# Second attention of a two-block network: the score products for the row maxima run for two heads at once, in two halves of TensorE's rows

## What is computed

```python
qkv = x @ Wqkv
q, k, v = jnp.split(qkv, 3, axis=-1)            # (4, 512, 256) each
q = q.reshape(b, s, 16, 16)                     # 16 heads of 16
q = q / (sqrt(mean(q * q)) + EPS) * scale_q     # one mean over everything
k = k / (sqrt(mean(k * k)) + EPS) * scale_k
attn = softmax(einsum('bqhd,bkhd->bhqk', q, k))
z = einsum('bhqk,bkhd->bqhd', attn, v)
x = x + z.reshape(b, s, 256) @ Wo
```

## Time and profile before

| | us |
|---|---|
| median of 3 runs | 1603.98 (1602.13 to 1608.87) |
| profiled execution | 1612.12, span 1610.3, mean granted TensorE clock 0.947 |
| busy: PE, PEld, DVE | 1461.8 (91%), 999.7, 1066.7 |
| busy: ACT, POOL | 855.1, 477.2 |
| first tall tile of rounds 0, 1, 2 | 938.00, 953.38, 966.78 |
| value products of round 1 begin at | 956.48, 959.75, 963.03, 965.78 |
| first tall tile of the last round, its last value products | 1149.89, 1161.75 |

### The profile page before, as it was taken

One profiled execution on the slowest core, in us unless ns is written; L12 is line 12 of the kernel. 1 busy time (PEld: TensorE's weight loads), 2 busy tenths in 40 slices (PEclk: granted clock), 3 DMA queues, 4 the chain that ended last, 5 costly groups with the idle time before them and its releaser, 6 DMA issues.

```text
span 1610.3 us, 20214 instructions
## 1 busy us (share of the span) xinstructions
PE 1461.8 (91%) x7408; PEld 999.7 (62%) x7420; DVE 1066.7 (66%) x1216; ACT 855.1 (53%) x1511; POOL 477.2 (30%) x140
## 2 busy tenths in 40 slices
PE   5898797589898999997999889999899999999997
PEld 3576342289797978753444333333368888888886
DVE  6996496579899898864443567777355565565655
ACT  2433466499889898631343268777624333333332
POOL 0999110069888888400321320000000000000000
PEclk7899899789999999979999999999978999999999
DMA  6110010402222111402112122442000000000000
GB/s 266 35 48 1 1 53 21 178 27 85 100 105 106 66 66 41 161 2 39 44 36 78 50 81 59 138 137 92 1 1 0 1 14 1 1 14 1 13 1 14
DMA packets 36624, 87.61 MB, mean 54 GB/s; under 512 B 8350, under 2 KB 24948, under 8 KB 32948
## 3 DMA queue, kind: packets, MB, share of 16 engines
q1 hardware_dynamic: 36532, 86.39, 16.1%
HBM read 68.10 MB, written 18.21 MB: 54 GB/s over the span
## 4 chain that ended last, share of the span: by engine, by line
PE 55%; ACT 2%; DVE 2%; issue 2%; DVEq 1%; ACTq 0%
PE ps L1418 13%; PE ps L1427 12%; PE ps L1288 4%; PE ps L1155 3%; PE ps L1330 3%; PE ps L1276 2%; PE ps L1181 2%; PE ps L1117 2%; ACT arena L1851 1%; PE ps L987 1%; PE ps L580 1%; PE ps L1313 1%; PE ps L1039 1%; PE ps L1189 1%; PE ps L1167 1%
## 5 line engine op out<-in xcount | busy, mean ns | idle before, releaser
L2500 POOL TENSOR_TENSOR arena<-arena 128x2048 f32<-128x2048 f32 x63 | 287.3, 4579 | 167.1 <-DVE arena L2059 166.8
L2059 DVE TENSOR_TENSOR_SCAN arena<-arena,ps 128x1024 f32<-128x1024 f32 x128 | 284.2, 2271 | 44.9 <-ACT arena L1694 22.3
L1418 PE MATMUL ps<-arena 128*128 128x256 f32 x896 | 216.7, 388 | 3.2 <-DVE early L2445 1.8
L1418 PEld LDWEIGHTS ps<-arena 128*128 128x128 f32 x896 | 173.1, 195 | 30.3 <-DVE early L2445 3.0
L1694 ACT ACTIVATE arena<-arena,mam 128x511 f32<-128x511 f32 x256 | 166.1, 712 | 34.3 <-DVE arena L2059 34.3
L1851 ACT ACTIVATE arena<-ps,rho 128x512 f32<-128x512 f32 x256 | 158.3, 689 | 27.7 <-PE ps L1330 26.5
L2291 DVE TENSOR_REDUCE mxs<-ps 128x1 f32<-128x512 f32 x224 | 141.1, 684 | 44.9 <-PE ps L1276 43.1
L975 PE MATMUL ps<-early,arena 128*128 128x128 f32 x768 | 129.7, 277 | 18.1 <-DVE arena L2059 17.8
L1884 ACT ACTIVATE hT<-hT,arena 128x256 f32<-128x256 f32 x192 | 85.5, 500 | 86.7 <-DVE hT L2449 55.1
L2480 POOL TENSOR_TENSOR arena<-arena 128x4096 f32<-128x4096 f32 x16 | 115.0, 7189 | 43.6 <-DVE arena L1978 43.6
L1682 ACT ACTIVATE arena<-arena,early 128x512 f32<-128x512 f32 x192 | 124.0, 711 | 0.1
(11 more groups left out here) (344 smaller groups left out, 2328.5 us busy)
## 6 DMA issues: line engine op xcount, KB each, us to landing
arena<-bc_scratch SPq DMA_DIRECT2D x32, 512.0 KB, 3.7
arena<-in_ffn SPq DMA_DIRECT2D x8, 1024.0 KB, 4.9
batch_scratch<-arena SPq DMA_DIRECT2D x2, 3072.0 KB, 9.1
arena<-batch_scratch SPq DMA_DIRECT2D x6, 1024.0 KB, 6.8
arena<-q_scratch SPq DMA_DIRECT2D x96, 64.0 KB, 2.2
arena<-k_scratch SPq DMA_DIRECT2D x96, 64.0 KB, 2.2
arena<-in_dec_w SPq DMA_DIRECT2D x1, 3855.0 KB, 16.4
arena<-in_cond SPq DMA_DIRECT2D x1, 3739.5 KB, 11.5
```

The costliest lines, as they stand in the source:

```text
L1418: done = pe.matmul(ps[:, bank, i * S // 2:(i + 1) * S // 2], weights[:, f, :], x, start=first and i == 0, stop=last and i == 1, skip_group ...
L2059: dve.tensor_tensor_scan(half, view(decay[:, (2 * k + h) % 3], [[1, 2 * S]]), view(ps[:, FEED + 2 * h, :], [[1, 2 * S]]), 0.0, ALU.mult, A ...
L2500: pool.tensor_tensor(state[:, k % SLOTS], state[:, k % SLOTS], view(c_rows[:, j % 2, k % G, :], [[0, M], [1, S]]), ALU.mult).then_inc(s_hc, 1)
```

## The change

- A short product takes three of the six part pairs, 48 rows (`MAIN`). Heads of even number have these in rows 0 to 47, heads of odd number in rows 64 to 111, so that two heads' products can stand in the two row halves of TensorE.
- The other three pairs lie in the other half, from row 65 for even heads and from row 1 for odd ones (`PART_ROWS`); the maxima's row is 64 for even heads and 0 for odd ones (`MAX_ROW`). A tall product takes rows 0 to 112 (`TALL` = 113), the gaps being zero.
- The three early stacks keep the old order, and all their pairs.
- In `attend` the order is two tall tiles, then both short ones, with one wait ahead of them: for the maximum two before the first of them.
- `load_heads` needs two DMAs for a block of 16 rows, one for the even and one for the odd heads: 24 for 12 in a stack, each of half the bytes. The maxima's row is two DMAs for one.
- GpSimd writes, for each of the four stacks in `qstack` and `kstack`, rows 32 to 63 and 96 to 127 with zeros in q and k, and the rows of -1 in k (`constant_rows`), after its split of the last k: first for the fourth group, for which SP now waits (`s_ones` 2) ahead of its load, then for the others, for which it waits (`s_ones` 5) ahead of the first load of batch 1.

```diff
+MAIN = 3 * DH
+TALL = P // 2 + 1 + MAIN
+MAX_ROW = (P // 2, 0)
+PART_ROWS = ((0, DH, 2 * DH, P // 2 + 1, P // 2 + 1 + DH, P // 2 + 1 + 2 * DH),
+             (P // 2, P // 2 + DH, P // 2 + 2 * DH, 1, 1 + DH, 1 + 2 * DH))
...
+        def is_early(b, hg):
+            return isinstance(b, int) and b == 0 and hg < 3
+
+        def heads_loaded(b, hg):
+            return len(Q_PARTS) * 2 * 16 * (2 * b + (1 if hg < 3 else 2))
...
+                    for odd in range(2):
+                        at = PART_ROWS[odd][j]
+                        queue.dma_start(of_parity(stack, odd)[at:at + DH],
+                                        bass.AP(src.tensor, src.offset + off + odd * DH * row,
+                                                [[row, DH], [2 * DH * row, HG // 2], [1, S]])
+                                        ).then_inc(s_heads[hg], 16)
...
-            sp.dma_start(stacks_of(0, 0)[0][STACK:STACK + 1], mrow[0:HG, 0, :]).then_inc(s_mrow_in, 16)
+
+            def max_rows_in(b, hg):
+                for odd in range(2):
+                    sp.dma_start(max_row_of(b, hg, odd), mrow[odd:HG:2, hg % 2, :]).then_inc(s_mrow_in, 16)
+
+            max_rows_in(0, 0)
             store_parts(B - 1)
+            sp.wait_ge(s_ones, 2)
             load_heads(sp, 0, HG - 1, Q_STACK, K_STACK)
...
                         if b == 0 and hg == 0:
                             sp.wait_ge(s_q_out, 16 * B + 1)
                             sp.wait_ge(s_k_out, 16 * B + 1)
+                            sp.wait_ge(s_ones, 5)
...
-                i, qc = s % HG, s // HG
+                qc = s // HG
                 if s == 0:
-                    pe.wait_ge(s_heads[hg], (b + 1) * 2 * len(Q_PARTS) * 16)
-                pe.wait_ge(s_max, (b * HG + hg) * 16 + s + (1 if hg + s == 0 else -1))
+                    pe.wait_ge(s_heads[hg], heads_loaded(b, hg))
+                pe.wait_ge(s_max, (b * HG + hg) * 16 + s + (1 if hg + s == 0 else 0))
                 q, k = stacks_of(b, hg)
-                pe.matmul(ps[:, (hg + s) % 3, :], q[0:STACK, i, qc * P:(qc + 1) * P], k[0:STACK, i, :],
-                          start=True, stop=True).then_inc(s_s_mm, 1)
+                for odd in range(2):
+                    i = s % HG + odd
+                    low = 0 if is_early(b, hg) else odd * P // 2
+                    rows_in = slice(low, low + (STACK if is_early(b, hg) else MAIN))
+                    pe.matmul(ps[:, (hg + s + odd) % 3, :], q[rows_in, i, qc * P:(qc + 1) * P], k[rows_in, i, :],
+                              start=True, stop=True).then_inc(s_s_mm, 1)
...
-                            pe.matmul(ps[:, 3 + (hg + n) % 3, :], k[0:STACK + 1, i, kc * P:(kc + 1) * P],
-                                      q[0:STACK + 1, i, :], start=True, stop=True).then_inc(s_t_mm, 1)
-                            if not (final and hg >= 2):
-                                scores(*ahead, n)
+                            tall = STACK + 1 if is_early(b, hg) else TALL
+                            pe.matmul(ps[:, 3 + (hg + n) % 3, :], k[0:tall, i, kc * P:(kc + 1) * P],
+                                      q[0:tall, i, :], start=True, stop=True).then_inc(s_t_mm, 1)
+                        if not (final and hg >= 2):
+                            scores(*ahead, 4 * kc + 2 * pair)
...
-            minus_row(kstack[:, HG - 1]).then_inc(s_ones, 1)
+                last = minus_row(stack)
+            last.then_inc(s_ones, 1)
             pool.drain()
             split_parts(pool, B - 1, kf, last_kp, rest_q, s_kf, s_k_out, s_kp)
-            for hg in range(HG - 1):
-                last = minus_row(kstack[:, hg])
-            last.then_inc(s_ones, 1)
+
+            def constant_rows(hg):
+                for low in (P // 4, 3 * P // 4):
+                    for stack in (qstack, kstack):
+                        pool.memset(view(stack[low:low + P // 4, hg], [[1, HG * S]]).bitcast(F32), 0.0)
+                for odd in range(2):
+                    at = MAX_ROW[odd]
+                    last = pool.memset(of_parity(kstack[:, hg], odd)[at:at + 1].bitcast(F32), minus_ones)
+                last.then_inc(s_ones, 1)
+
+            pool.wait_ge(s_qp, B + 1)
+            constant_rows(HG - 1)
+            pool.wait_ge(s_vs, B + 1)
+            pool.wait_ge(s_q_out, 16 * B + 1)
+            pool.wait_ge(s_k_out, 16 * B + 1)
+            for hg in range(HG - 2):
+                constant_rows(hg)
+            constant_rows(HG - 2)
```

More of the change, by code:

```diff
@@ L467, in stacks_of, with of_parity, max_row_of @@
         def stacks_of(b, hg):
-            if isinstance(b, int) and b == 0 and hg < 3:
+            if is_early(b, hg):
                 return early_q[hg], early_k[hg]
             return qstack[:, hg], kstack[:, hg]
+        def is_early(b, hg):
+            return isinstance(b, int) and b == 0 and hg < 3
+        def heads_loaded(b, hg):
+            return len(Q_PARTS) * 2 * 16 * (2 * b + (1 if hg < 3 else 2))
+        def of_parity(stack, odd):
+            return stack.rearrange("p (j o) s -> p j o s", o=2)[:, :, odd]
+        def max_row_of(b, hg, odd):
+            at = STACK if is_early(b, hg) else MAX_ROW[odd]
+            return of_parity(stacks_of(b, hg)[0], odd)[at:at + 1]
         va, at = carve(at, TILES, H * SLOT)
@@ L631, in load_heads @@
                     off = (hg % 2) * HG * DH * row + part * C * S + (hg // 2) * S
-                    queue.dma_start(stack[j * DH:(j + 1) * DH],
-                                    bass.AP(src.tensor, src.offset + off, [[row, DH], [DH * row, HG], [1, S]])
-                                    ).then_inc(s_heads[hg], 16)
+                    if is_early(b, hg):
+                        queue.dma_start(stack[j * DH:(j + 1) * DH],
+                                        bass.AP(src.tensor, src.offset + off, [[row, DH], [DH * row, HG], [1, S]])
+                                        ).then_inc(s_heads[hg], 16)
+                        continue
+                    for odd in range(2):
[3 more added lines that the diff above has]
+                                                [[row, DH], [2 * DH * row, HG // 2], [1, S]])
+                                        ).then_inc(s_heads[hg], 16)
         @block.sync
@@ L772, in feed @@
                         sp.wait_ge(s_mrow, g + 3)
-                        row = stacks_of(b + (hg + 1) // HG, nxt)[0]
-                        sp.dma_start(row[STACK:STACK + 1], mrow[0:HG, nxt % 2, :]).then_inc(s_mrow_in, 16)
+                        max_rows_in(b + (hg + 1) // HG, nxt)
                     if not last:
@@ L1322, in attend @@
                     ahead = (b + (hg + 2) // HG, (hg + 2) % HG)
-                    pe.wait_ge(s_mrow_in, 16 * (g + 1) + 1)
+                    pe.wait_ge(s_mrow_in, 32 * (g + 1) + 1)
                     for j in range(8):
@@ L1368, in _ @@
             attend(0, True, False)
-            pe.wait_ge(s_ones, 2)
+            pe.wait_ge(s_ones, 5)
             with pe.Fori(1, B - 1) as b:
@@ L1839, in max_row @@
                 act.wait_ge(s_m_tr, g + 1)
-                act.wait_ge(s_mrow_in, 16 * g - 15)
+                act.wait_ge(s_mrow_in, 32 * g - 31)
                 act.activation(mrow[:, parity, :], ps[0:HG, 7, :], ACT.Copy).then_inc(s_mrow, 1)
@@ L2529, in _ @@
             for stack in early_k:
-                minus_row(stack)
-            minus_row(kstack[:, HG - 1]).then_inc(s_ones, 1)
+                last = minus_row(stack)
+            last.then_inc(s_ones, 1)
             pool.drain()
             split_parts(pool, B - 1, kf, last_kp, rest_q, s_kf, s_k_out, s_kp)
-            for hg in range(HG - 1):
-                last = minus_row(kstack[:, hg])
-            last.then_inc(s_ones, 1)
+            def constant_rows(hg):
[14 more added lines that the diff above has]
+            constant_rows(HG - 2)
             pool.drain()
```

## The result

The changed kernel takes 1619.93 us (median of 10 runs, 1611.52 to 1632.17), the kernel before 1603.76 (10 runs, 1599.94 to 1608.87): ratio 1.0103, 95% interval 1.0073 to 1.0133. It is slower by 16 us.

What follows compares the result with a forecast made beforehand. In the second attention, ScalarE bounds each round's first and last quarters, TensorE the middle two. Start stall 6.5, half clock 2.0 and steady rounds 2.7 sum to +11.2 us on 1604.0: 1615.2, 8 in 10 within 1606 to 1627.

Steps and rivals of the forecast that it cites:

- The likeliest case: Whole kernel: start stall, half clock and slower steady rounds add 11.2 us, giving 1615.2; chance 0.52, own range 1610 to 1621.
- The start stall: Second attention, before round 1: SyncE waits for GpSimd's constants, then issues 24 DMAs, so the first tall product starts 6.5 us later.
- The stage is the same in both: Step from profiled execution (1612.1 us) to median run (1604.0): the second attention was taken as equal, so 11.2 us was added unchanged.
- Half clock in round 1: Round 1 of the second attention, after TensorE's idle time: clock at 0.50 adds 2.0 us, from 0 to 2.4.
- Steady: Rounds 3 to 15 of scores: joint wait for maxima and 0.09 us edges add 0.23 us a round, 2.7 us in all.
- Later rows of maxima: Later rounds of the second attention: SyncE's longer loads stay hidden; rows 0.2 late in two rounds, at most 0.5 us, taken as 0.
- The slack of 0.8 us: SyncE's queue in later rounds: load and maxima row take 15.1 us, 15.9 are available, so at least 0.8 us remains.
- the rival with 0.62: SyncE's loads: each issue costs 0.62 us, SyncE becomes the bound, +20 us, 1639; chance 0.06.
- one after the other: Short-product pairs on TensorE: the two halves run in sequence, not side by side, +11.4 us, 1626.6; chance 0.13.
- Edges free: TensorE between full and half rows: shape changes cost nothing, -5.3 us in the rounds, 1607.2 in all; chance 0.16.
- the cheaper start: Start of the second attention: half loads issue in 0.36 us and the clock holds for half, 1611.6; chance 0.09.
- the full gain: TensorE's short products: 22.7 us less, with 8.5 us lost at the start, comes through, 1589.8; chance 0.04.

Runs made afterwards that it cites:

- half_alone: Changed kernel in the old order, tall and short products alternating, each 48-row short product alone with its own wait: 1654.7 us, ratio 1.0317 to the kernel before.
- before_again: The kernel before, unchanged, run for a second trace: its profiled execution took 1600.10 us.
- split_loads: The kernel before with only the change's DMAs: 24 of 32 KB for 12 of 64 KB per stack, two per maxima row: 1614.1 us, ratio 1.0044.
- order_only: The kernel before with only the new order, two tall products, then two full 96-row short ones behind one joint wait: 1602.1 us, ratio 0.9988.
- order_soft: The kernel before in the order tall, tall, short, short, each short product waiting only for its own bank: 1605.2 us, ratio 0.9966.
- mended: Changed kernel with batch 0's fourth stack in old form, constant waits per stack, maxima rows sent before a load's last four DMAs: 1604.6 us, ratio 1.0020.
- half_max: Changed kernel with VectorE's maxima taken over 256 of the 512 score columns: 1616.1 us, ratio 1.0067 to the kernel before.
- after_again: The changed kernel, unchanged, run for a second trace: 1619.7 us.

## Why the prediction was right

Forecast 1615.2, range 1606 to 1627, slower 0.68; measured 1619.9. The likeliest case was the one that came, 4.7 us short. Of the signs named as right, all came: SyncE's 24 issues (942 to 954, in an execution whose stage began 4 us sooner), the gap ahead of T0 of round 1, half clock behind it, pairs within 0.03, 0.31 at the edges, pairs 1.17 apart, rounds of 13.6 to 13.7. One of the signs named as wrong came too, waits of T0 on a DMA in later rounds.

- **The start stall, +6.5.** Right in kind and, by its own trace, in size: T0 of round 1 was to come 18.8 us after the store of k and came 19.2 after, 0.9 of that from one issue of 1.35 us. Mis-sized is what it was measured against. T0 of round 1 is now set by POOL and SyncE alone, whatever TensorE does in round 0 (half_alone: 22.53 us at full clock, after: 22.35 partly at half clock). The trace of before had 2.5 us of half clock in round 0 (15.39 against 12.91 in before_again); in an execution without them the stall costs 9.4. "The stage is the same in both" was the step that didn't hold.
- **Half clock in round 1, +2.0.** Round 1 is 2.9 over, 2.6 of that beyond the steady 0.3. In the other traces with a stall in front of round 1 that round is 1.6 us over (split_loads) to 4.3 (half_alone); before, before_again, order_only, order_soft and mended, without a stall, have round 1 at full clock.
- **Steady, +0.23 a round.** Measured +0.30 in rounds 2, 3, 6 and 10, +0.16 to +0.24 in 4, 5, 9 and 11, next to nothing in 8 and 13, each behind a late row, and 2.8 over the 13 rounds without the waits for rows, 2.7 predicted. (13 times 0.23 is 3.0; the sum of the prediction says 2.7, which is a slip.) By stretch, with the prediction in brackets: T0 to V0 +0.20 in rounds 2 and 3, +0.12 in 6, 7, 10 and 11 (+0.13), +0.07 where ScalarE also copies the normalised z (+0.05), V0 to V1 +0.18 (+0.17), V1 to V2 -0.08 (-0.07), with the projection +0.08 (+0.09). order_only, half_max and half_alone show both causes by themselves: the joint wait, and 0.10 us an edge (0.09 taken). One term under them was too low: without the wait a pair comes round in 0.95 us (half_max), not in 0.86. It cost nothing here, since the wait of 1.17 lies over it.
- **Later rows of maxima, 0.** Wrong in size: rounds 7 and 12 are 0.59 and 0.88 us longer by it, 1.5 in all. The slack of 0.8 us was too large on three counts. The working names 0.4 us from the start of T15 to the start of the load and leaves them out. It takes 2.2 us from the row's issues to T0, where behind a piece of the expert weights it was 3.4 to 4.1 in the 17 later waits for such a row in all these traces, and 1.06 without weights; the prediction had seen this landing and set it to 0. And it takes each issue at its median: the earlier trace rows held maxima of 1502 ns for the loads and 943 for the weights that I passed over. Ahead of the late row of round 8 a load's issue took 1.17 us, ahead of that of round 13 the weights' issue 1.30. The long issue alone does not make a row late: in after_again one of 1.49 us stands ahead of the row of round 5, without weights, and T0 did not wait; in split_loads T0 of round 12 waited 0.12 us behind weights with no long issue at all.
- **GpSimd's constants, 4.5:** 4.8. **Issues at 0.468 whatever the size:** 0.466 (median step) for half the bytes, 0.469 in before; the rival with 0.62 falls. **Within a pair 0.02:** under 0.01; the rival "one after the other" falls. **Edges free** falls with half_alone; the cheaper start falls with the 0.466, and the full gain with the median.

The sum of before's profiled trace to after's: 7.0 + 2.9 + 2.5 (rounds 2 to 13) + 1.5, less 1.4 in round 14, which ran at half clock only in before: 12.5, and the stage grew by 12.46 (223.75 to 236.21). Against before_again it is 16.3, and the medians are 16.2 apart; that these two agree may be luck, as what lies outside the stage differs by several us from one execution to the next. At the same granted clock it is 10.7. I read this last as lower because part of the damage is the clock, which that figure takes out; no run separates the two. What share of the 16.2 us is chance of the clock in stages that the change doesn't touch stays open: ten runs of after don't settle it, and against the other medians of before, up to 1610.5, the changed kernel would be 9.5 slower.

## What to carry to other kernels

A product over part of TensorE's rows is worth its edges only in a run of them: with two tall products between pairs, one edge in and one out cost 0.2 us (half_alone), which is what the pair saves. When rows of a buffer are rearranged, count what its loads and its constants issue on the queue behind which a small, urgent transfer stands, take the longest issue seen and not the median, and look at what large transfer stands just ahead of it; and when a stall is taken away, ask which wait it had covered. Hold executions against each other at the same granted clock, or the clock decides the verdict: order_only has 0.5 us more in nearly every round and the median of before.

## What the runs showed of the hardware

- Two products over rows 0 to 47 and 64 to 111, into different banks, take 0.39 us together as one does alone. The Trainium skill (TensorE: Matmul & The Clock Gate, Part 3) gives some 4 ns between starts in different row tiles. The trace agrees: 3 or 4 ns in 104 pairs.
- 48 rows to 113 and back: 0.10 us each way, bf16 to bf16.
- A DMA takes 0.466 us of SyncE's queue for 32 KB and 0.469 for 64 KB, and lands in 1.8 and 2.2 us. Now and then a single issue takes 0.9 to 1.9 us (four of 312 of the loads in the changed kernel's first trace, two of 156 in before's); what makes it do so was not found.
- A row of maxima of 2 KB lets T0 start 1.06 us after its issue has ended, and 3.4 to 4.1 us where 1024 KB were issued just ahead of it on the same queue, at most 0.7 us behind the landing of those.
- GpSimd sets 32 x 1024 words in 0.93 us, one row of 1024 in 0.91.
